# Expert layers of a small language-model tower: padded tiles of picks against unpadded blocks kept in a ring

## The reference

```python
# layer 0: 8 experts, 2 picks a token, hidden width 512
probs = softmax(xf @ Wr + br); vals, idx = top_k(probs, 2)
for e in range(8):
    out += cw[:, e, None] * (relu(xf @ W1[e] + b1[e]) @ W2[e] + b2[e])
# layer 1: 8 groups of 8 experts, 2 groups and in each 2 experts a token, hidden width 256
h = relu(einsum('td,gedh->tgeh', xt, W1) + b1)
y = einsum('tgeh,gehd->tged', h, W2) + b2
out = einsum('tgd,tg->td', einsum('tged,tge->tgd', y, c2), c1)
```

## Time and profile before

| | |
|---|---|
| median of 3 runs | 1232.41 us (1230.72 to 1233.87) |
| span of the profiled execution | 1313.1 us; the page gives no other time of it |
| busy: PE, PEld, DVE, ACT, POOL | 785.0, 616.5, 767.4, 411.7, 610.2 us |
| mean granted TensorE clock | 0.749 of 2.4 GHz |
| gathers of rows for the tiles (line 741) | 264, 254.0 us busy |

### The profile page before, as it was taken

How to read it: one execution, slowest core, us unless ns; L and a number is a source line. 1 busy time by engine, 2 the same in 40 slices (tenths; PEclk the granted TensorE clock), 3 DMA queues, 4 the chain that set the end, 5 groups by cost and what they waited for, 6 DMA issues and landing times.

```text
span 1313.1 us, 18765 instructions
## 1 busy us (share of the span) xinstructions
PE 785.0 (60%) x4730; PEld 616.5 (47%) x4731; DVE 767.4 (58%) x2226; ACT 411.7 (31%) x1129; POOL 610.2 (46%) x638
## 2 busy tenths in 40 slices
PE   0206964979996277876776135777788878510000
PEld 0105453779996143443456013666677677410000
DVE  6894266656664348888666997444454455533321
ACT  2364241524443233342014046333333333100000
POOL 7852000255552546552000037665555565577773
PEclk9998975579999557666655555899999999655555
DMA  2480069012222285747003031333332359322221
GB/s 67 142 334 0 1 198 322 0 47 72 66 70 49 71 148 120 156 108 134 8 0 118 5 116 28 76 86 74 82 80 78 86 75 76 57 68 62 68 60 37
DMA packets 110519, 113.15 MB, mean 86 GB/s; under 512 B 17107, under 2 KB 95762, under 8 KB 110226
## 3 DMA queue, kind: packets, MB, share of 16 engines
q1 hardware_dynamic: 94796, 80.61, 22.5%
q0 software_dynamic: 15680, 32.05, 13.1%
HBM read 81.06 MB, written 31.51 MB: 86 GB/s over the span
## 4 chain that ended last, share of the span: by engine, by line
PE 44%; DVE 25%; issue 10%; POOL 9%; another core or an unknown queue 5%; DMA 3%; ACT 3%; SPq 1%; DVEq 1%; POOLq 0%; ACTq 0%
PE ps L524 13%; PE ps L530 11%; POOL zbuf L762 9%; DVE zbuf L1138 5%; PE ps L1703 4%; DVE zbuf L1041 3%; DVE bnst L816 2%; PE ps L1873 2%; PE ps L520 2%; PE ps L1914 2%; PE ps L1967 1%; ACT xbuf L1501 1%; DMA zbuf<-xrows,holder 1%; DVE mv L819 1%
## 5 line engine op out<-in xcount | busy, mean ns | idle before, releaser
L741 POOL DMA_INDIRECT zbuf<-xrows,holder x264 | 254.0, 962 | 196.5 <-PE ps L520 143.9
L762 POOL DMA_INDIRECT zbuf<-results,place x192 | 186.2, 970 | 111.5 <-issue 54.1
L524 PE MATMUL ps<-zbuf,tbuf 128*128 128x128 f32 x1340 | 211.3, 291 | 43.7 <-DVE zbuf L451 29.7
L530 PE MATMUL ps<-big,zbuf 128*128 x1328 | 210.5, 291 | 18.5 <-issue 13.2
L524 PEld LDWEIGHTS ps<-zbuf,tbuf 128*128 128x128 f32 x1340 | 178.6, 200 | 60.2 <-DVE zbuf L451 36.9
L530 PEld LDWEIGHTS ps<-big,zbuf 128*128 128x128 f32 x1328 | 175.3, 198 | 29.7 <-issue 26.9
L451 DVE COPY zbuf<-ps 128x128 f32<-128x128 f32 x264 | 76.9, 291 | 190.7 <-PE ps L524 112.0
L492 ACT ACTIVATE zbuf<-ps,tbuf 128x128 f32<-128x128 f32 x335 | 115.3, 366 | 196.7 <-PE ps L524 99.2
L1138 DVE TENSOR_REDUCE zbuf<-ps 125x3 f32<-125x1500 f32 (+1 forms) x96 | 143.7, 1540 | 46.6 <-PE ps L1703 44.6
L1703 PE MATMUL ps<-big 97*125 97x500 bf16 x256 | 105.5, 548 | 39.9 <-DVE zbuf L1138 31.8
L1117 DVE SCALAR_TENSOR_TENSOR h<-zbuf,gate,h 125x128 f32<-125x128 f32 x152 | 52.3, 352 | 108.7 <-DMA zbuf<-results,place 92.3
(11 more groups left out here) (362 smaller groups left out, 1165.3 us busy)
## 6 DMA issues: line engine op xcount, KB each, us to landing
results<-zbuf SPq DMA_DIRECT2D x130, 128.0 KB
big<-kappa SPq DMA_DIRECT2D x8, 1750.0 KB, 21.0
big<-parts SPq DMA_DIRECT2D x96, 125.0 KB
big<-in_L_ffn_W_dram SPq DMA_DIRECT2D x10, 1024.0 KB, 9.3
big<-in_L_ffn_W_dram SPq DMA_DIRECT2D x64, 128.0 KB, 2.7
parts<-zbuf SPq DMA_DIRECT2D x24, 250.0 KB
zbuf<-xrows,holder POOLq DMA_INDIRECT x264
xrows<-xbuf SPq DMA_DIRECT2D x2, 1792.0 KB
```

Of the source, the lines that this page charges most:

```text
L524: last = t.matmul(ps[:, (2 if k < c.HC // 2 else 4) + u % 2, 128 * k:128 * k + 128], ring.w1[u % U][:, 128 * k:128 * k + 128], ring.rT[u % ...
L530: last = t.matmul(ps[:, 6 + u % 2, 0:D], ring.hid[u % 2][:, 128 * k:128 * k + 128], w2v[:, bass.ds(e, 1), k, :].rearrange("p e d -> p (e d ...
L741: gp.indirect_dma_start(ring.rows[tau % RING], None, xrows[:, :], bass.IndirectOffsetOnAxis(ap=holder[:, tau:tau + 1], axis=0)).then_inc(S ...
L762: gp.indirect_dma_start(got[n % 8], None, results[f][:, :], bass.IndirectOffsetOnAxis(ap=place[f][:, k, t:t + 1], axis=0)).then_inc(S(f"go ...
```

## The change

The picks are sorted by expert without padding, and cut into blocks of 128: 63 in layer 0, 125 in layer 1. A block that holds picks of several experts is computed once for each of them, so a tile is a pair of block and expert, and with E experts there are at most blocks + E - 1 tiles: 70 and 188. A tile's block is its number less its expert's. A block is gathered and transposed once and kept transposed in a ring of 16 blocks (layer 0) or 67 blocks (layer 1), which TensorE addresses by a register. The first tiles of a layer turn blocks, the last E tiles or so don't. `table` now holds the expert of a tile in 6 bits and, in 8 more, whether each next tile has the next expert; both engines load it every 8 tiles. `holder` and `hot_tile` are 128 wide (`HOLD`) for 192. VectorE copies a block when it is turned, ahead of its wait for `first`.

```diff
-        full = (NT * R * picks + 127 * self.E) // 128
-        self.tiles = -(-full // U) * U
+        self.blocks = -(-NT * R * picks // 128)
+        self.tiles = self.blocks + self.E - 1
+        self.full = (self.blocks - 2) // RING
...
+TAB = FFN[1].tiles + 16
+HOLD = 128
+SPAN = 16384
+KEEP = {0: 16, 1: 67}
...
-        def tile_experts(eng, c, tau):
-            packed = eng.value_load(table[c.n][0:1, bass.ds(tau, 1)], min_val=0, max_val=c.E ** U - 1)
-            bits = c.E.bit_length() - 1
-            return [(packed >> bits * u) & (c.E - 1) for u in range(U)]
+        def tile_experts(eng, c, tau, n):
+            packed = eng.value_load(table[c.n][0:1, bass.ds(tau, 1)], min_val=0, max_val=64 * 256 - 1)
+            e = [packed & 63]
+            for i in range(n - 1):
+                e.append(e[-1] + ((packed >> (6 + i)) & 1))
+            return [nc.s_assert_within(n, 0, c.E - 1, skip_runtime_bounds_check_because="the table holds numbers of experts") for n in e]
+
+        def kept_at(c, j):
+            j = nc.s_assert_within(j, 0, 2 * KEEP[1] - 1, skip_runtime_bounds_check_because="a tile's expert is not over the tile's number")
+            if c.n == 0:
+                return j & 15
+            return nc.s_assert_within(j - KEEP[1] * ((j + (128 - KEEP[1])) >> 7), 0, KEEP[1] - 1,
+                                      skip_runtime_bounds_check_because="a block's number is under twice the ring")
```

On VectorE the tiles become:

```diff
+            def tiles(first_tile, count, turns):
+                for u in range(count):
+                    if u < turns:
+                        dve.wait_ge(S(p + "turned"), first_tile + (u + 3))
+                        turn(u, first_tile + (u + 2))
+                    if u == 0:
+                        experts = tile_experts(dve, c, first_tile + 3, count)
+                    dve.wait_ge(S(p + "hid_filled"), first_tile + (u + 4))
                     rectify(u + 1)
-                    if u == 0:
-                        experts = tile_experts(dve, c, i * U + 3)
                     stage(experts[u], u + 3)
```

and on TensorE, with POOL's gathers last:

```diff
-            def tiles(first_tile, count):
+            def tiles(first_tile, count, turns):
                 for u in range(count):
-                    pe.wait_ge(S(p + f"row_ld{(u + 2) % RING}"), (first_tile + (u + 2) // RING * RING) * (16 // RING) + 16)
-                    turn(u + 2)
-                    pe.wait_ge(S(p + "rT_ready"), first_tile + (u + 4))
-                    first(u + 1)
-                    if u % U == 0:
-                        experts = tile_experts(pe, c, first_tile + u)
+                    if u < turns:
+                        pe.wait_ge(S(p + f"row_ld{(u + 2) % RING}"), (first_tile + (u + 2) // RING * RING) * (16 // RING) + 16)
+                        turn(u + 2)
+                        pe.wait_ge(S(p + "blocks_in"), first_tile + (u + 2))
+                    if u == 0:
+                        experts = tile_experts(pe, c, first_tile, count + 1)
+                        if turns == 0:
+                            pe.wait_ge(S(p + "blocks_in"), c.blocks)
+                    pe.wait_ge(S(p + "w1_ready"), first_tile + (u + 4))
+                    first(u + 1, first_tile + (u + 1) - experts[u + 1])
                     pe.wait_ge(S(p + "hid_dve"), first_tile + (u + 3))
                     pe.wait_ge(S(p + "hid_act"), first_tile + (u + 3))
-                    second(experts[u % U], u)
-            with pe.Fori(0, c.tiles // RING) as i:
-                tiles(i * RING, RING)
-            tiles(c.tiles // RING * RING, c.tiles % RING)
+                    second(experts[u], u)
+            with pe.Fori(0, c.full) as i:
+                tiles(i * RING, RING, RING)
+            tiles(c.full * RING, RING, c.blocks - 2 - c.full * RING)
+            if c.tiles // RING > c.full + 1:
+                with pe.Fori(c.full + 1, c.tiles // RING) as i:
+                    tiles(i * RING, RING, 0)
+            tiles(c.tiles // RING * RING, c.tiles % RING, 0)
...
-                for tau in range(c.tiles + 2):
+                for j in range(c.blocks):
```

In `route`, a short scan over the experts (`sofar`) comes behind the long one; the steps that rounded the counts and summed them (`ntile`), and the product `ends` with its copy, go; the comparison `over` moves ahead of the slots. A slot is kept as 16384 times the expert plus the place among the sorted picks, so two more sets of small steps follow the look-up of the slots:

```diff
-                me.then(v.scalar_tensor_tensor(pair[:, 0:TAB - 1], one[:, 1:TAB], float(c.E), one[:, 0:TAB - 1], ALU.mult, ALU.add))
-                me.then(v.scalar_tensor_tensor(table[f][:, 0:n], pair[:, 2:n + 2], float(c.E ** 2), pair[:, 0:n], ALU.mult, ALU.add))
+                me.then(TT(out=steps[:, 0:n + 7], in0=one[:, 1:n + 8], in1=one[:, 0:n + 7], op=ALU.subtract))
+                for w in (1, 2, 4):
+                    k = n + 7 - w if w == 1 else n + 7 - 3 if w == 2 else n
+                    me.then(v.scalar_tensor_tensor(steps[:, 0:k], steps[:, w:w + k], float(2 ** w), steps[:, 0:k], ALU.mult, ALU.add))
+                me.then(v.scalar_tensor_tensor(table[f][:, 0:n], steps[:, 0:n], 64.0, one[:, 0:n], ALU.mult, ALU.add))
...
-                me.did(v.tensor_copy(place[f][0:R, 0:c.K, :], sm[:, 0:c.K, :]))
+                me.then(TS(of, sm[:, 0:c.K, :], (SPAN - 1) / 2.0, 1.0 / SPAN, ALU.subtract, ALU.mult))
+                me.then(TS(of, of, MAGIC, None, ALU.add))
+                me.then(TS(of, of, MAGIC, None, ALU.subtract))
+                me.then(v.scalar_tensor_tensor(sm[:, 0:c.K, :], of, -float(SPAN), sm[:, 0:c.K, :], ALU.mult, ALU.add))
+                me.then(v.scalar_tensor_tensor(place[f][0:R, 0:c.K, :], of, 128.0, sm[:, 0:c.K, :], ALU.mult, ALU.add))
```

More of the change, by code:

```diff
@@ L163, in tower_kernel @@
         h = sb("h", [R, NT, D])
-        xbuf = sb("xbuf", [128, NT * D])
+        wide = sb("wide", [128, 3 * NT * D])
+        xbuf, tbuf, zbuf = (wide[:, n * NT * D:(n + 1) * NT * D] for n in range(3))
         x = xbuf[0:R, :].rearrange("p (t d) -> p t d", t=NT)
-        tbuf = sb("tbuf", [128, NT * D])
-        zbuf = sb("zbuf", [128, NT * D])
         xT = tbuf[:, 0:NT * R].rearrange("p (t r) -> p t r", t=NT)
@@ L345, in __init__ @@
             def __init__(self, c):
-                o = 0
+                o = 128 * KEEP[1] if c.n else NT * D
                 def take(n, w):
                     nonlocal o
-                    r = [zbuf[:, o + w * i:o + w * i + w] for i in range(n)]
+                    r = [wide[:, o + w * i:o + w * i + w] for i in range(n)]
                     o += n * w
+                    assert o <= 3 * NT * D
                     return r
[L352 to L355, removed]
+                self.blocks = wide[:, 0:128 * KEEP[c.n]].rearrange("p (k t) -> p k t", t=128)
+                self.w1 = take(U, c.wcols)
+                o = max(o, 2 * NT * D)
+                self.rows, self.hid = take(RING, 128), take(2, 128 * c.HC)
+                self.res = take(RING, 128)
+                self.res2 = [wide[:, o - 256 * n:o - 256 * n + 256].rearrange("p (o d) -> p o d", o=2) for n in range(RING // 2, 0, -1)]
         block = ctx.enter_context(nc.Block())
@@ L520, in turn, with first @@
                 t.transpose(ps[:, u % 2, 0:128], ring.rows[u % RING], ident).then_inc(S(p + "turned"), 1)
-            def first(u):
+            def first(u, block):
+                turned = ring.blocks[:, 0, :] if block is None else                     ring.blocks[:, bass.ds(kept_at(c, block), 1), :].rearrange("p k t -> p (k t)")
                 for k in range(c.HC):
                     last = t.matmul(ps[:, (2 if k < c.HC // 2 else 4) + u % 2, 128 * k:128 * k + 128], ring.w1[u % U][:, 128 * k:128 * k + 128],
-                                    ring.rT[u % U], start=True, stop=True)
+                                    turned, start=True, stop=True)
                 last.then_inc(S(p + "hid_filled"), 1)
@@ L1946, in _ @@
                 pe.wait_ge(S(q + "counted"), 3)
-                p = use(f"ends{f}")
-                filled(t.matmul(p[0:c.E, 0:1], ltri[0:c.E, 1, 0:c.E], ncolb[0:c.E, :], start=True, stop=True))
-                pe.wait_ge(S(q + "counted"), 4)
                 p = use(f"expert{f}")
```

126 lines of the change are left out of this document (64 added, 62 removed).

## The result

The changed kernel takes 1241.91 us (median of 4 runs, 1239.12 to 1243.06), the kernel before 1232.89 (4 runs, 1230.72 to 1233.87): ratio 1.0076, 95% interval 1.0056 to 1.0096. It is slower by 9.0 us; the forecast was 11 us faster. The profiled execution of after takes 1242.67 us with a span of 1240.9.

A forecast was written before the change was run, and what follows sets the result against it. The array was taken to bind layer 0, and the array and TensorE's sequencer meeting on load tiles to pace layer 1. Terms -11.5 - 5.7 - 3.4 + 3.3 + 1 + 5 = -11.3 gave 1221 us, range 1176 to 1280.

The forecast's parts named there:

- the price of a tile in layer 1: TensorE's sequencer in layer 1: 1.37 us a tile with a transpose, 1.25 without, against 1.39 before; -11.5 us.
- The pace of before: Layer 1 of the kernel before: 1.39 us a tile net of unknown waits, 257.3 us over 185 steps.
- The frame: Whole kernel: the profile's 80.7 us over the median left aside, its time difference taken off the median unchanged.
- Rival A: TensorE's tiles, mainly layer 1: more register work than counted, +40 to +61 us there; 1262 to 1289 us; chance 0.29.
- B: Layer 1: the array sets the pace and hides the register work, -63 us, 1170 us; chance 0.17.
- C: Layer 1: a tile stays at 1.39 us, +0.0 there, the rest the same, 1232 us; chance 0.11.
- D: Tiles without transposes: the clock falls to 1.2 GHz, +29 us, 1250 us; chance 0.06.
- the saved records: Layer 0: fewer tiles and transposes save 54 matmul records, -5.7 us if the array goes on binding.
- Cold code: Written-out tiles and a second loop run for the first time in both layers: +5 us, bounds 0 and 24.
- Routing: Table and block computations before the tiles: layer 0 +1.5, layer 1 +1.8, together +3.3 us; bounds 2 and 6.
- The table of 128: Table of picks 128 wide for 192: 0.21 us less a group in layer 0, -3.4 us; layer 1 nothing.
- The end: `late_gates` gets four more instructions, 2.2 us, ahead of the first combination: +1 us, bounds 0 and 2.2.

The follow-up runs named there:

- undisturbed profile: The kernel before, unchanged, run and profiled again on a chip where it takes 1232 to 1233 us: 1236.82 us, span 1235.1.
- the variants: The changed kernel without a block address, with the table load moved earlier, or with 16-tile loops: 1273.91, 1284.99, 1286.36 us where the kernel before takes 1320.5.
- The load ahead: The changed kernel with TensorE's table load moved to the middle of the loop before, its bounds check replaced by a register copy: 1221.8 us, ratio 0.9899.
- loops of 16: The changed kernel with loops of 16 tiles in place of 8 on TensorE and VectorE: 1225.59 us, ratio 0.9945.
- spread row numbers: The kernel before, with layer 1's gathers from tile 158 on taking row numbers of filled tiles: 1219.34 us, ratio 0.9892.
- the variant with all three edits: The changed kernel with 16-tile loops, the table load in the loop before, and the wrap left out where the tile's number decides: 1201.76 us, ratio 0.9753.

## Why the prediction was wrong

**The step that failed** is the price of a tile in layer 1: "0.99 + 0.35 = 1.34, and I take **1.37** for a tile with a transpose". It measured 1.477, and 1.283 instead of 1.25 without a transpose: 121 x 0.107 + 64 x 0.033 = 15 us, of the 22 by which layer 1 missed. Moved together with the pace of before (1.273), a tile with a transpose went +0.20 where I had -0.02. The sequencer's register and semaphore instructions in 16 tiles of after, by line (551 is the block's address, 557 that of W2, 583 and 586 are waits):

```profile
L551 PEldq ALU_OP  x36: 32/36/36, 874.6 to 895.8; - x36
L551 PEldq FUSED_REGOPS  x32: 42/132/232, 875.0 to 896.2; - x32
L557 PEldq FUSED_REGOPS  x32: 46/56/70, 875.6 to 896.6; - x32
L583 PEldq ALU_OP  x16: 32/36/36, 874.5 to 895.6; - x16
L586 PEldq EVENT_SEMAPHORE  x16: 51/51/51, 875.5 to 896.3; - x16
```

Away from a loop's start that is eight a tile, where I had ten: the six of before and two FUSED_REGOPS, but no second EVENT_SEMAPHORE and no further ALU_OP. One of the two multiplies for the wrap and takes 0.22 us, 0.28 to the next instruction, where I had 0.11 for each. The two errors about cancel: 0.28 + 0.10 for 4 x 0.11. What failed is the overlap. I took the pace for the sum of the sequencer's steps, plus 0.03, as soon as that sum is above the array's time. But inside a loop a tile takes 1.30 us, where that sum without load and branch is 1.20, and the first tile of a loop adds 0.17 a tile where I had 0.7/8 + 0.45/8 = 0.14. The eight instructions of one such tile start within 1.0 us (864.10 to 865.07). Then the sequencer stands still to 865.6, while the array works. From there to 866.2 it works out the next address, and the array's last matmul before that starts at 865.79. So `first` comes with a gap:

```profile
866.27 0.71 PE L551 MATMUL ps<-wide 128*128 x4 [0.21 <-issue]
```

Each waits for the other in turn; what holds the sequencer in the 0.5 us was not taken apart. The runs do show what the work costs as it stands: all of the address 0.23 us a tile (1.477 to 1.249), the wrap 0.13, a loop's start about 1.4 us.

**The pace of before** was the second. "Net of them a tile of layer 1 takes 257.3 / 185 = 1.39 us": the sum nearly held, 251.2 undisturbed, which is 6 us of the 22; the last 1 lies in the first three steps. The one pace did not hold. It is a mean of some 160 tiles at 1.27 and the last 28, which are empty, at 1.84. That loads add to the array's time was right: of eight steps undisturbed five take 1.10 and the three around loads and branch 1.3, 1.6 and 1.8. But the 15 us that the change gains from the empty tiles' gathers were inside the mean, so the change seemed to gain by tiles that it makes slower. The pace of the first profile could not tell, as its last 28 steps take 1.54 us, no more than its mean of 1.60. Its page could: its row of DMA shares has one slice of nine tenths late in layer 1. In the undisturbed profile, with GB/s under it:

```profile
DMA  3390049202223167657500403134444369422222
GB/s 68 100 403 5 1 145 324 85 24 60 70 68 69 44 149 142 129 123 142 95 1 0 126 5 96 48 91 103 102 106 104 104 82 67 60 62 70 63 67 61
```

Engines that are full at 67 GB/s, where 104 took four tenths, are a stretch of its own. **The frame** failed too: the 80.7 us were not waits that lie on top of both kernels alike. On such a chip more than half of them (52 of 84 us) sit in layer 1, with the tiles that gather (1.6 for 1.27), of which the change removes 65, and the variants lose less there than before does.

**The rivals.** Rival A named this mechanism, more register work, and its condition (from 0.06 us a tile on; 0.107 came). Its size, 40 to 61 us for 13, was three times too large or more, and its reasons (an address for each product, pieces that don't fuse) were not the ones. B, C and D are out: no stretch of after is near the array's 1.10 with a transpose, the time moved, and the clock stayed at its upper level.

**Layer 0 hides only a part.** It hid the work of a tile, 1.895 back to back, but not a loop's start. I spread the load over 8 tiles and compared means; at a start the sequencer works for 2.2 us in one piece, from the branch (353.0) to `first` (355.2), and the array runs dry. Six starts at 2.8 us and two at 2.3, instead of 1.895, are the 6 us that took back the saved records (-5.7 forecast, -0.4 measured). The load ahead shows it: -5.8. Some luck is in the -0.4: the first two steps of the layer are 2.1 us shorter in after, which no term of mine holds.

**Cold code** (+5) did not show; the first copies of layer 0, my row for its high end, are as slow in before and faster in after, and loops of 16 cost nothing that shows. My row for the +5 was misread twice: 1.57 a tile was no slower than that profile's 1.60 (I held it against the net 1.39), and those seven tiles are empty ones; with spread row numbers the last steps take 1.10 to 1.78 like all others. **Routing** was +0.9 for +1.5 in layer 0. **The table of 128** gave -1.6 for -3.4: half the groups left the chain for a copy of ScalarE. **The end** is +0.3 for +1 (and four instructions at my own prices are 1.9 us, not 2.2). In the profiles the miss is 17 us, +5.9 for -11.3: layer 1 +22.4 and layer 0 +5.3, against -5 for the cold code and -4.9 for the stage between the layers, whose -3.1 lies within what one profile leaves open.

The Trainium skill, "TensorE: Matmul & The Clock Gate", section "Wait — 56ns, not 53.3ns?", gives about 62 ns of the sequencer for each MATMUL when hardware decode is off; with it on, by the same section, a MATMUL doesn't use the sequencer. Which was set here no run shows. The price with it off does not fit this trace either: in the last tiles of the variant with all three edits (line 568, 1000.41 and 1000.55), two FUSED_REGOPS with a product's two matmuls between them start 0.14 us apart, and two ALU_OPs with none between them 0.10.

## What to carry to other kernels

Before a mean pace is used as what a change is measured against, split the stage until the steps are alike; a slice where the DMA engines are full at few GB/s marks a stretch of its own. A count of the sequencer's instructions is not a pace, even where it comes out above the array's time. Register work on TensorE's sequencer is hidden by the work queued ahead of it, not by the mean of a loop: a load with its check belongs behind a product that needs nothing of it, one loop early if need be, and an address is cheapest where the loop's bounds decide it. Padded entries of a gather should point to different rows.

## What the runs showed of the hardware

A gather whose 128 row numbers are all the same held the DMA engines at a share of 0.96 and came at 1.84 us, against 0.36 to 0.41 and 1.27 with rows that differ. A FUSED_REGOPS with the multiply of the wrap takes 0.22 us, others 0.04 to 0.08, an ALU_OP 0.036, a TENSOR_LOAD 0.30 and its bounds check 0.15 to 0.17, a COMPARE_BRANCH 0.21. And the same kernel takes 1320.5 us on one chip and 1232 to 1233 on three others; in layer 1 the difference sits in tiles that gather, 1.62 for 1.27. The cause was not found.
